# A four-layer block on one core: score units in pairs, flat attention rows, a full-height third gate matmul, new orders of pieces

## The reference

```
x += gate3(gn(x))     three sigmoid gates (over C, H, W) of max and mean maps, 7x7 convolutions,
                      mixed by a softmax over channel logits
x += conv3x3(gn(x))   weights: a mixture of circulant projections
x += gn(x) * w        w: squeeze and excitation of a low-pass mean
x += roll(attention(windows(roll(gn(x), -4))), 4)
                      64 windows of 8x8 pixels per image, 8 heads, relative bias, shift mask
```

## Time and profile before

| | us |
|---|---|
| median of the runs shown | 2861.73 |
| profiled execution, span from first to last instruction | 2861.8 |
| busy: PE, DVE, ACT, POOL | 2343.5, 2302.6, 1658.0, 1404.0 |
| first convolution ends, last convolution ends | 333, 2642 |
| image in the middle: convolution end to convolution end | 327 |

### The profile page before, as it was taken

The page is one execution under the profiler, slowest core; times in us unless marked ns, Lnnn a source line. Parts: engine busy times, 40 slices in busy tenths (PEclk is TensorE's granted clock), DMA queues, the critical chain, the costliest instruction groups (busy, mean ns, idle before and its releaser), DMA issues. The chain is left out here.

```text
span 2861.8 us, 68259 instructions
## 1 busy us (share of the span) xinstructions
PE 2343.5 (82%) x27252; PEld 1322.5 (46%) x27252; DVE 2302.6 (80%) x4579; ACT 1658.0 (58%) x4200; POOL 1404.0 (49%) x1132
## 2 busy tenths in 40 slices
PE   0367649898889969898798978899798978899887
PEld 0323225444544545445554545444454545544554
DVE  8887957879887887878887887878888787878665
ACT  1322057645865577644875567744866468745665
POOL 3315542456635572456625574455724565354454
PEclk9959869999999999999999999999999999999999
DMA  5400400023110230014001231014100240001111
GB/s 148 122 0 17 169 1 32 16 89 119 39 39 31 90 104 32 31 54 154 31 31 38 87 114 32 31 38 152 49 32 16 89 133 32 32 30 53 53 61 39
DMA packets 90338, 176.14 MB, mean 62 GB/s; under 512 B 37526, under 2 KB 50470, under 8 KB 80422
## 3 DMA queue, kind: packets, MB, share of 16 engines
q1 hardware_dynamic: 90022, 171.77, 18.1%
HBM read 98.86 MB, written 72.86 MB: 60 GB/s over the span
## 5 line engine op out<-in xcount | busy, mean ns | idle before, releaser
L2020 PE MATMUL F<-g_raw,cw_hi 128*128 128x512 f16 x2304 | 695.2, 384 | 50.0 <-DVE ytj L1447 12.8
L878 POOL TENSOR_TENSOR xs<-xs,rec 128x512 f32<-128x512 f32 x256 | 290.1, 1134 | 674.3 <-DVE rec L1795 671.1
L1157 ACT ACTIVATE xs<-xs,mx 128x64 f32<-128x64 f32 x1792 | 448.1, 335 | 115.1 <-DVE mx L1790 114.5
L2020 PE MATMUL F<-g_raw,cw_lo 128*128 128x512 f16 x1152 | 441.3, 383 | 0.0
L2020 PEld LDWEIGHTS F<-g_raw,cw_hi 128*128 128x128 f16 x2304 | 220.0, 98 | 317.7 <-issue 19.1
L1779 DVE TENSOR_TENSOR xs<-SP,bias 128x512 f32<-128x512 f32 (+2 forms) x384 | 182.5, 503 | 110.8 <-PE SP L2111 110.1
L863 POOL TENSOR_TENSOR tmp<-X,uw 128x512 f32<-128x512 f32 x128 | 162.8, 1282 | 210.2 <-DVE X L1635 122.0
L1164 ACT ACTIVATE prt<-PTR 128x512 f32<-128x512 f32 x256 | 151.1, 590 | 192.5 <-PE PTR L2121 174.1
L1368 DVE SCALAR_TENSOR_TENSOR g_raw<-l0c,gn,g_raw 128x512 f16<-128x512 f32 x192 | 192.1, 1043 | 54.5 <-ACT g_raw L1015 42.2
L2079 PE MATMUL QP<-tok_hi,qkv_hi 128*128 128x512 f16 x470 | 186.4, 397 | 48.9 <-ACT qq L1138 28.2
L1794 DVE TENSOR_REDUCE sums<-xs 128x8 f32<-128x512 f32 x256 | 173.1, 676 | 46.2 <-ACT xs L1157 22.9
(11 more groups left out here) (322 smaller groups left out, 5757.4 us busy)
## 6 DMA issues: line engine op xcount, KB each, us to landing
scratch_x<-X SPq DMA_DIRECT2D x32, 1024.0 KB, 6.2
xs<-scratch_x SPq DMA_DIRECT2D x56, 512.0 KB, 3.6
out_x<-xs SPq DMA_DIRECT2D x56, 512.0 KB, 2.8
X<-in_x SPq DMA_DIRECT2D x25, 1024.0 KB, 6.4
l0c<-scratch_t SPq DMA_DIRECT2D x8, 1876.0 KB, 11.9
l0c<-in_x SPq DMA_DIRECT2D x7, 1024.0 KB, 5.7
l0c<-scratch_t SPq DMA_DIRECT2D x8, 640.0 KB, 14.4
l0c<-scratch_t SPq DMA_DIRECT2D x8, 576.0 KB, 15.4
```

What stands on the lines that cost most here:

```text
L878: G.tensor_tensor(keyed(sc[:, u % 4, :]), keyed(sc[:, u % 4, :]), rec[:, u % 4, :].unsqueeze(2).to_broadcast([P, 8, TOK]), ALU.mult).then_ ...
L1157: last = S.activation(keys, keys, ACT.Exp, bias=mx[:, u % 4, i:i + 1])
L2020: last = T.matmul(F[:, n % 2, :], wgt[:, ci, C3 * comp + dx, P * co:P * co + P], win[which], start=(ci == 0 and dx == 0 and j == 0), stop= ...
```

## The change

**Score units in pairs.** `scores` and `total` take two units at once: one addition over both banks of `SP` (or two additions, where the row's last window has a bias of its own), one maximum, one sum and one reciprocal over 1024 columns and 16 groups. All counts go up by two. ScalarE and GpSimd still take single units.

```
-                    dve.wait_ge(s_done, u + 1)
+                    dve.wait_ge(s_done, u + 2)
...
-                    V.tensor_reduce(mx[:, buf, :], keyed(sc[:, buf, :]), AX.X, ALU.max, negate=True).then_inc(s_max, 1)
+                    V.tensor_reduce(mx[:, buf:buf + 2, :].rearrange("p a k -> p (a k)"),
+                                    sc[:, buf:buf + 2, :].rearrange("p a (k m) -> p (a k) m", m=TOK), AX.X, ALU.max,
+                                    negate=True).then_inc(s_max, 2)
...
-                    dve.wait_ge(p_exp, u + 1)
-                    seq.link(V.tensor_reduce(sums[:, u % 4, :], keyed(sc[:, u % 4, :]), AX.X, ALU.add))
-                    V.reciprocal(rec[:, u % 4, :], sums[:, u % 4, :]).then_inc(p_rec, 1)
+                    dve.wait_ge(p_exp, u + 2)
+                    seq.link(V.tensor_reduce(both(sums), sc[:, buf:buf + 2, :].rearrange("p a (k m) -> p (a k) m", m=TOK),
+                                             AX.X, ALU.add))
+                    V.reciprocal(both(rec), both(sums)).then_inc(p_rec, 2)
```

```
+            lo = W * (WS * (row % NW) + SHIFT)
+            if row % NW < NW - 1:
+                return [(0, CHUNK - SHIFT, lo + SHIFT), (CHUNK - SHIFT, SHIFT, lo)]
...
-                    S.activation(dst[:, :, 0:W - SHIFT], src[:, :, SHIFT:W], ACT.Identity, **kw)
-                    S.activation(dst[:, :, W - SHIFT:W], src[:, :, 0:SHIFT], ACT.Identity, **kw).then_inc(tok_set, 1)
+                    S.activation(tok[:, t, :], xr[:, r % 3, t, :], ACT.Identity, bias=c_b3[:, t:t + 1],
+                                 scale=c_a3[:, t:t + 1]).then_inc(tok_set, 1)
...
-                    for to, at_, n in ((SHIFT, 0, W - SHIFT), (0, W - SHIFT, SHIFT)):
-                        last = V.scalar_tensor_tensor(img[:, :, to:to + n], out_rows[:, :, at_:at_ + n], out_scale,
-                                                      img[:, :, to:to + n], ALU.mult, ALU.add)
-                    last.then_inc(qp_taken, 1)
-                    wait_read(dve, f"p{co}.{r}")
-                    V.memset(sm[:, 3, :], 0.0).then_inc(x4_set, 1)
+                    row = xr[:, r % 3, co, :]
+                    V.scalar_tensor_tensor(row, bank(FILL[f"p{co}.{r}"]), out_scale, row, ALU.mult,
+                                           ALU.add).then_inc(p_added, 1)
+def wrapped():
+    i, j = np.divmod(np.arange(TOK), WS)
+    return (i + (j >= SHIFT)) % WS * WS + j
```

```
+                        if f == "hwgate":
+                            pool.wait_ge(f_sum, at(f_sum, PAIRS))
+                            G.memset(tmp[:, 0:2, :], 0.0).then_inc(srow_zero, 1)
...
+                    if t == rows == 1:
+                        G.memset(flat, 0.0).then_inc(srow_zero, 1)
...
-                        T.matmul(F[:, k % 2, :], ones3[:, :], srow[:, CHUNK * k:CHUNK * k + CHUNK], start=True,
+                        T.matmul(F[:, k % 2, :], ones3[:, :], srow_all[:, CHUNK * k:CHUNK * k + CHUNK], start=True,
...
-                            T.matmul(F[:, n % 2, :], w3t[:, P * t:P * t + P], srow[:, px], start=False,
+                            T.matmul(F[:, n % 2, :], w3t[:, P * t:P * t + P], srow_all[:, px], start=False,
```

**New orders.** Every table is replaced. A line of `TURN` for VectorE, as an example:

```
-        "hwrows": "SS", "band0": "STK", "band1": "S", "band2": "ATK", "bandcopy": "AT", "hwmean6": "T",
+        "reduce12": "KTA", "reduce13": "K", "reduce14": "A", "reduce15": "UUTUU", "hwrows": "SS", "band0": "T",
```

More of the change, by code:

```diff
@@ L262, in build @@
         tmp = sb("tmp", [P, 4, CHUNK])
-        srow = tmp[0:3, :, :].rearrange("p a b -> p (a b)").bitcast(fp16)
+        srow_all = tmp[:, :, :].rearrange("p a b -> p (a b)").bitcast(fp16)
+        srow = srow_all[0:3, :]
         tok = sb("tok", [P, CT, CHUNK])
@@ L421, in build @@
         setup_end = sem("setup_end")
+        setup_perm = sem("setup_perm")
         pads_zero = sem("pads_zero")
@@ L501, in build @@
         ALONE = FILL[f"q0.{ENDING}"]
-        BY_DVE = [name for name in FILLS if name[0] == "p" or name[0] == "v" and int(name.split(".")[1]) >= ENDING]
-        BY_ACT = [name for name in FILLS if name not in BY_DVE]
+        ADDED = [name for name in FILLS if name[0] == "p"]
+        BY_DVE = [name for name in FILLS if name[0] == "v" and int(name.split(".")[1]) >= ENDING]
+        BY_ACT = [name for name in FILLS if name not in ADDED and name not in BY_DVE]
         def bank(n):
@@ L734, in load @@
                     pool.memset(zrow[:, :], 0.0)
+                    pool.memset(w3t[:, :], 0.0).then_inc(pads_zero, 1)
                     pool.memset(neg_half[:, :], -0.5)
@@ L1332, in setup @@
                     dve.wait_ge(bias_rev_in, 16 * HEADS * WS)
-                    for y in range(4):
-                        if y:
-                            yield "bias"
-                        for hs in range(2):
-                            for cg in range(CT):
-                                last = V.tensor_tensor(bias[:, y, hs, cg, :], bias_rev[:, hs, cg, ::-1], mask[:, y, :], ALU.add)
+                    heads_of = lambda ap: ap.rearrange("p s t m -> p (s t) m")
+                    cells = lambda ap: ap.rearrange("p h (i j) -> p h i j", j=WS)
+                    for y in (0, 2):
+                        V.tensor_tensor(heads_of(bias[:, y, :, :, :]), heads_of(bias_rev)[:, :, ::-1],
+                                        mask[:, y, :].unsqueeze(1).to_broadcast([P, 2 * CT, TOK]), ALU.add)
+                    yield "bias"
+                    dve.wait_ge(setup_perm, 1)
+                    for y in (1, 3):
+                        dst = cells(heads_of(bias[:, y, :, :, :]))
+                        src = cells(PTR[:, 0:2 * CT * TOK].rearrange("p (h m) -> p h m", m=TOK)[:, :, ::-1])
+                        part = mask[:, y, :].rearrange("p (i j) -> p i j", j=WS).unsqueeze(1).to_broadcast([P, 2 * CT, WS, WS])
+                        for i, j, n, at_ in ((0, 0, WS, 0), (0, SHIFT, WS - 1, 1), (WS - 1, SHIFT, 1, 0)):
+                            last = V.tensor_tensor(dst[:, :, i:i + n, j:j + SHIFT], src[:, :, at_:at_ + n, j:j + SHIFT],
+                                                   part[:, :, i:i + n, j:j + SHIFT], ALU.add)
                     last.then_inc(setup_end, 1)
@@ L1777, in add_bias @@
                     def add_bias(w0, w1_, kind):
-                        span = slice(w0, w1_)
                         return V.tensor_tensor(
-                            sc[:, buf, :].rearrange("p (g w m) -> p g w m", g=CT, w=4)[:, :, span, :],
-                            SP[:, hs, :].rearrange("p (g w m) -> p g w m", g=CT, w=4)[:, :, span, :],
-                            bias[:, kind, hs, :, :].unsqueeze(2).to_broadcast([P, CT, w1_ - w0, TOK]), ALU.add)
+                            windows(sc[:, buf:buf + 2, :])[:, :, w0:w1_, :], windows(SP[:, :, :])[:, :, w0:w1_, :],
@@ L1784, in scores @@
+                            bias[:, kind, :, :, :].rearrange("p s t m -> p (s t) m").unsqueeze(2)
+                            .to_broadcast([P, 2 * CT, w1_ - w0, TOK]), ALU.add)
                     if quad == 0:
-                        add_bias(0, 4, low).then_inc(s_biased, 1)
+                        add_bias(0, 4, low).then_inc(s_biased, 2)
                     else:
                         add_bias(0, 3, low)
-                        add_bias(3, 4, low + 1).then_inc(s_biased, 1)
-                    dve.wait_ge(s_biased, u + 1)
@@ L1825, in score_units @@
                 def score_units():
-                    for u in range(4 * ROWS_ALL):
+                    for u in range(0, 4 * ROWS_ALL, 2):
                         scores(u)
@@ L1871, in setup @@
                     yield "value shift"
+                    pe.wait_ge(bias_rev_in, 16 * HEADS * WS)
+                    T.matmul(PTR[:, 0:2 * CT * TOK], wrap[:, :], bias_rev.rearrange("p s t m -> p (s t m)"), start=True,
+                             stop=True).then_inc(setup_perm, 1)
+                    yield "wrapped table"
                 def front(img):
@@ L1927, in front @@
                     pe.wait_ge(f_sum, at(f_sum, PAIRS))
+                    if img:
+                        pe.wait_ge(coef_set, img)
                     for i in range(2 * DJ):
@@ L2181, in shift_mask @@
     mask = np.where(kinds[:, :, None] != kinds[:, None, :], -100.0, 0.0).astype(np.float32)
+    for y in (1, 3):
+        mask[y] = mask[y][np.ix_(wrapped(), wrapped())]
     return np.concatenate([mask.transpose(1, 0, 2)] * 2, axis=0)
```

92 lines of the change are left out of this document (48 added, 44 removed), and 138 rows, old and new, of tables (FIRST, TURN).

## The result

The changed kernel takes 2847.9 us against 2861.7 before: the ratio of the compared runs is 0.9938, with a 95% interval of 0.9911 to 0.9966. (A fourth run of it took 3568 us at a granted clock of 0.65 and isn't compared.) It is faster by 0.6%, where 2.6% were forecast. The profiled execution has a span of 2843.1 us, 18.7 less than before, where 74.5 less were forecast.

The account below looks back on a forecast made before the run. TensorE was taken to bound gates and convolution, chains led by VectorE the rest. Savings of 9.2 us for each of seven images (64), 3 in the first and 7.5 in the last rows gave 2861.8 - 74.5 = 2787 us; range 2725 to 2852.

Parts of the forecast that it names:

- I take the reordering by itself at nothing: New piece orders on the engines: no cost or gain by themselves, bounds 3 us an image either way.
- The third matmul: Gates: its weight load waits because of another row count; 128 rows save 0.19 us each, 3.0 us an image.
- The rival that the row count doesn't matter: Gates: the row count isn't what holds the weight load, so 8 x 3.0 come back: 2811 us; chance 0.06.
- VectorE's prices: Paired and flat instructions: maxima 1197 ns, additions 1231, 957 and 731, reciprocals 210; together 15.1 us less VectorE work an image.
- Half of VectorE's savings on the path: Outside gates and convolution: half of the 8.0 us saved on VectorE comes through, 4.0 us an image.
- the sum for a middle image: Middle image: 3.0 + 4.0 + 0.7 + 1.5 = 9.2 us saved.
- The stretches: Middle image: VectorE gains outside gates and convolution, convolution gaps 1.5 us shorter.
- the 26 named as a sign: Gates of a middle image: a stretch near 26 us would show the forecast right.
- The row's extra transfer: One more DMA each way per row, landing after about 1.8 us, hidden by three buffers: cost nothing.
- The pairs' coupling: Slower rival: a pair's first unit reaches GpSimd and the turn 2.5 us later; 2907 us, chance 0.08.
- The last rows: After the last convolution: VectorE loses 15.1 us over eight rows, half counts, 7.5 us saved.

Follow-up runs that it names:

- orders_alone: Changed kernel with single units, two passes, small fill, third matmul over 3 rows without zero fills: nearly the work of the kernel before, under the new orders; 2950.3 us.
- tail_single: Changed kernel with scores and totals of the last eight rows as single units, two in the place of each pair, order as changed; 2843.7 us.
- tail_before: As tail_single, with the last rows' pieces on all engines in the order of the kernel before; 2815.6 us.
- second_sums: tail_before with 14 of 28 pieces of GpSimd's sums for the second image moved from ahead of its norm to their later-image places; 2812.6 us.
- second_sums_first_before: second_sums with the first image's order of the kernel before as well; 2801.8 us, ratio 0.9788.
- first_before: Changed kernel with the first image's pieces in the order of the kernel before, except pieces the new bias table alters; 2847.8 us.
- flat_alone: Kernel before with the flat rows alone (one token pass, one addition, no small fill, bias tables, two transfers per row), every order as before; 2838.3 us.

## Why the prediction was wrong

The step that failed is "I take the reordering by itself at nothing; the bounds are 3 us an image either way". It was argued from the number of pieces in each stretch, which says nothing of how a piece stands to the one that it waits for. The prediction gave the last rows and the first two images no term for the orders at all, and 49 of the 56 us of the miss lie there.

What the orders cost depends on the lengths that are played in them. With the old lengths (orders_alone) it is 7.4 us a middle image, outside the bounds, 24.3 in the last rows and 17.6 up to the end of the second convolution. With the new lengths the last rows show it, 24.4 us between tail_single and tail_before, and the first two images: 14.3 us at the end of the second convolution between second_sums and second_sums_first_before, though the first image's order alone, in first_before, moved that end by 1.4. For a middle image with the new lengths no run shows it. With both places mended the second convolution ends at 670.4 us, where the forecast had 667 (679.4 - 3 - 9.2), and the time of 2801.8 us is 15 over the forecast instead of 61, with single units in the last rows.

Point by point:
- The third matmul: the mechanism was right, to 0.01 us in the timeline. The size was 2.7 us in the gates and 2.1 in the length of an image, instead of 3.0. The rival that the row count doesn't matter is ruled out: the Trainium skill (TensorE: Matmul & The Clock Gate, LDWEIGHTS) has the cost in the columns alone, and the load itself agrees (92 and 101 ns), but the wait ahead of it, 60.9 us against 16.2, doesn't. The section of the Trainium skill that the prediction names for loads pulled ahead (same page, Step-by-step: what each phase is for) has a second condition beside the row groups, a load into the background weight buffer. No row here shows which of the two held; but loads of 128 rows, which meet other loads of 128 rows, wait only 1.9 us in 128 for their turn, so the row groups alone can't be the rule here.
- VectorE's prices: right, each within 2% but for the reciprocal (253 ns, 210 assumed). What those groups lose is 14.7 us an image, 15.1 forecast. Its busy time in an image went down by 8.6 only, from 272.82 to 264.20: 3.8 us came back in an untouched step, the subtraction of the token's high half, which the new order puts beside GpSimd's work. In the six middle images 77 of 96 of these run beside GpSimd for more than half of their time, and take 1126 ns on the mean; 18 have GpSimd idle and take 683. Before, it was 18 of 96 beside it. Lines before, then changed:

```profile
L1764 DVE TENSOR_TENSOR tok_lo<-tok,tok_hi 128x512 f16<-128x512 f32 x16 | 12.6, 796 | 0.8 <-ACT tok_hi L1123 0.7
```

```profile
L1787 DVE TENSOR_TENSOR tok_lo<-tok,tok_hi 128x512 f16<-128x512 f32 x16 | 16.4, 1023 | 0.6 <-ACT tok_hi L1138 0.5
```

- Half of VectorE's savings on the path: the sum for a middle image, 9.2 us, was near the 8.0 measured, but as the difference of two larger numbers, 15.4 gained by the parts and 7.4 lost by the orders. That it fitted is luck, and no proof of the half.
- The stretches: the image's beginning is 5 us shorter and `reduce` 3, where the gain was looked for, the convolution 1 (1.5 forecast). The gates take 30 us and not the 26 named as a sign, since the new order plays two more fills between them; what comes behind is that much shorter.
- The row's extra transfer, taken at nothing: four pixels a channel land after 3.5 us, where 1.8 was assumed:

```profile
xs<-scratch_x SPq DMA_DIRECT2D x64, 4.0 KB, 3.5
```

  In the line of ScalarE's token pass above, 19.2 us are waits for a row's load, one in each image from the second on. The kernel before and flat_alone have none, orders_alone has 17.2 us, so they come from the place of the loads in the new orders. Whether they lengthen an image isn't shown.
- The pairs' coupling, the rival on the slower side: no run shows that it costs anything. In the middle images the pairs are worth 7.6 us under the new orders.
- The last rows: 7.5 us less were forecast, half of what pairs and flat rows take off VectorE. In tail_before it is 7.8 us (219.7 -> 211.9), but with single units, and flat_alone has 3.4; that the numbers agree is luck. In the changed kernel the order turned it round.

## What to carry to other kernels

Where every engine plays its pieces strictly in a written order, an order can be fitted to the lengths of the pieces, as here, where the new orders cost 7.4 us an image with the old lengths: price the order as a term of its own, and hold it against the change by running the new order with the old pieces and one new piece in the old order. Look first at the stretches that have one kind of work only, the beginning and the end, where a wait has little other work to hide behind: here they held 49 of the 56 us. A middle stretch that comes out as forecast doesn't vouch for the sum.

## What was not expected of the hardware

VectorE slows beside GpSimd, but not in every instruction: a pass of 1152 columns with one input from SBUF took 2297 ns instead of 818, a subtraction of two inputs 1023 instead of 796 in the middle images, and statistics (684 and 679) didn't change. The Trainium skill (SBUF — State Buffer, SBUF: two separate sides) has the two engines share one pair of ports by an exclusive lock, which VectorE needs with two inputs from SBUF or in a faster mode of two ports; these rows are in line with it, though none shows which instruction runs in such a mode. GpSimd's idle time in the set-up was therefore not free. Rows moved in two transfers of 508 and 4 KB, with 125431 packets instead of 90338, cost nothing that flat_alone shows, which has 125432 of them and is 23 us faster than the kernel before.
